# Shared expert of three token groups computed in the drain of the attention, and the whole shared expert in plain fp32

## The reference, cut to what matters

```python
def _L1_ffn_ref(hidden_tensor, w_router, w1_stack, w2_stack, ws1, ws2):
    ...   # two experts of eight for each token, weighted: moe_out
    sh = jnp.square(jax.nn.relu(jnp.einsum('btc,fc->btf', hidden_tensor, ws1)))
    shared_out = jnp.einsum('btf,cf->btc', sh, ws2)
    return shared_out + moe_out
...
t = t + _L1_ffn_ref(_ln_t(t), L1_ffn_w_router, L1_ffn_w1_stack, L1_ffn_w2_stack, L1_ffn_ws1, L1_ffn_ws2)
```

## Time and profile before

| what | value |
|---|---|
| median of three runs | 1196.7 us |
| profiled execution | 1199.71 us |
| its span, first to last instruction | 1197.3 us |
| mean granted clock of TensorE, share of full speed | 0.920 |
| PE busy, matmuls | 1025.8 us (86%) |
| DVE busy | 615.7 us (51%) |
| ACT busy | 528.2 us (44%) |
| POOL busy | 264.1 us (22%) |
| DMA | 114.61 MB, mean 96 GB/s |

### The profile page before, as it was taken

One profiled execution on the slowest core, in us unless ns is written; L12 is line 12 of the kernel. 1 busy time (PEld: TensorE's weight loads), 2 busy tenths in 40 slices (PEclk: granted clock), 3 DMA queues, 4 the chain that ended last, 5 costly groups with the idle time before them and its releaser, 6 DMA issues. The chain is left out here.

```text
span 1197.3 us, 19835 instructions
## 1 busy us (share of the span) xinstructions
PE 1025.8 (86%) x5686; PEld 858.5 (72%) x5686; DVE 615.7 (51%) x1712; ACT 528.2 (44%) x1328; POOL 264.1 (22%) x274
## 2 busy tenths in 40 slices
PE   6956669999999999973489999998776799997897
PEld 6956658888888888862256665665535799986787
DVE  5488653323232322226356676555778355554566
ACT  6027264444444444432144344433335466666563
POOL 0000012111111111107522200000000554424655
PEclk9999999999999999995689999997665799998889
DMA  9533501111111111118222301002230344434444
GB/s 354 234 110 136 176 24 49 53 54 54 54 54 53 54 54 54 49 41 268 73 80 79 89 1 53 36 18 71 89 123 1 101 139 140 136 114 150 151 131 132
DMA packets 63237, 114.61 MB, mean 96 GB/s; under 512 B 9827, under 2 KB 43253, under 8 KB 62262
## 3 DMA queue, kind: packets, MB, share of 16 engines
q1 hardware_dynamic: 49910, 77.65, 18.5%
q0 software_dynamic: 12960, 35.41, 10.4%
q10 hardware_dynamic: 288, 0.47, 0.1%
HBM read 73.90 MB, written 39.59 MB: 95 GB/s over the span
## 5 line engine op out<-in xcount | busy, mean ns | idle before, releaser
L574 POOL DMA_INDIRECT experts_rows_sb<-h_rows,ids_i x142 | 134.6, 948 | 751.0 <-POOLq L402 423.1
L761 DVE TENSOR_TENSOR experts_a_sb<-experts_a_sb,experts_bankU 128x512 f32<-128x512 f32 x71 | 48.9, 689 | 224.1 <-PE experts_bankU L180 224.1
L714 ACT ACTIVATE experts_a_sb<-experts_bankG 128x512 f32<-128x512 f32 (+1 forms) x142 | 70.0, 493 | 93.0 <-PE experts_bankG L180 91.2
L705 ACT ACTIVATE experts_hT<-experts_bankH 128x256 fp32r<-128x256 f32 x142 | 54.5, 384 | 89.6 <-PE experts_bankH L634 89.5
L727 ACT ACTIVATE experts_y_sb<-experts_bankY 128x256 f32<-128x256 f32 x142 | 54.8, 386 | 87.7 <-PE experts_bankY L177 65.3
L178 PE MATMUL attn_bankC<-attn_padded,attn_w_high 128*128 128x512 f32 x144 | 76.4, 530 | 19.8 <-ACT attn_feat L1432 14.6
L1136 POOL DMA_INDIRECT attn_y<-y_rows,pos_i x64 | 63.9, 998 | 112.2 <-DVE x_res L1562 57.2
L834 POOL DMA_INDIRECT shared_y<-y_rows,pos_i x64 | 65.4, 1022 | 63.9 <-DVE x_res L943 32.1
L177 PE MATMUL experts_bankY<-down_plain,experts_aT_plain 128*128 x284 | 72.9, 379 | 0.0
L183 DVE TENSOR_TENSOR experts_aT<-experts_bankA,experts_aT 128x256 fp32r<-128x256 f32 x142 | 59.6, 420 | 24.1 <-ACT experts_aT L722 24.1
L641 PE MATMUL experts_bankA<-konst_sb,experts_a_sb 128*128 128x128 f32 x426 | 70.0, 273 | 0.4 <-DVE experts_aT L183 0.4
(11 more groups left out here) (365 smaller groups left out, 2853.5 us busy)
## 6 DMA issues: line engine op xcount, KB each, us to landing
y_rows<-experts_y_sb SPq DMA_DIRECT2D x142, 128.0 KB, 1.7
h_rows<-xn SPq DMA_DIRECT2D x32, 256.0 KB, 2.4
x_res<-in_x SPq DMA_DIRECT2D x4, 1024.0 KB, 12.3
mix_xT<-in_xt SPq DMA_DIRECT2D x4, 1024.0 KB, 14.1
gate_raw<-in_L_ffn_gate_w SPq DMA_DIRECT2D x1, 4096.0 KB, 14.2
up_raw<-in_L_ffn_up_w SPq DMA_DIRECT2D x1, 4096.0 KB, 23.5
x_rows<-x_res SPq DMA_DIRECT2D x16, 256.0 KB
x_res<-x_rows SPq DMA_DIRECT2D x8, 512.0 KB, 4.6
```

The lines of the kernel that those rows point to most:

```text
L574: nc.gpsimd.indirect_dma_start(rows[t % DEPTH][:, :], None, h_dram, bass.IndirectOffsetOnAxis(ap=ids_i[:, t:t + 1], axis=0)).then_inc(s_ro ...
L714: nc.scalar.activation(a_sb[i % RING][:, :], bankG[i % RING][:, 0:hidden], ACT.Silu if gate is not None else ACT.Relu).then_inc(s["act"], 1)
L761: nc.vector.tensor_tensor(a_sb[i % RING][:, :], a_sb[i % RING][:, :], bankU[i % RING][:, 0:hidden], ALU.mult).then_inc(s["a"], 1)
```

## The change

- PE, ACT and DVE compute the shared expert of pairs 4, 5 and 6 (`EARLY`) inside `attention`. In iteration i PE multiplies the turned rows of pair i-5, which lie in `xT` for the router, by `ws1` (`shared_up`, four chunks, in banks that the attention no longer uses), ACT takes relu and square (`activate_shared`), and in iteration i+1 PE multiplies back (`shared_down`, four tiles) and DVE adds the result to `x_res` in two halves (`add_shared`). This falls into iterations 9 to 12. Their rows aren't stored to `ht_dram`.
- `ws1` and `ws2` are loaded as they are by two DMAs in iteration 8 and never split; 16 pieces are left, and `SHARES` falls to one in each of iterations 10 to 12.
- `shared` does the other five groups. All its products are single plain fp32 matmuls; there is no high or low half of rows, weights or activations. The five groups of rows have a buffer each and are loaded at the start. There are 16 gather buffers. The tiles are gathered, summed and stored in the order of groups 4, 0, 1, 5, 2, 6, 3, 7; a tile of an early group needs only its two sums.

```diff
+GROUP = 4
+EARLY = (4, 5, 6)
 ...
         def shared(ws1, ws2):
-            GROUPS = TILES // GROUP
+            LATE = [g for g in range(TILES // GROUP) if g not in EARLY]
+            SEQUENCE = [t for g in (4, 0, 1, 5, 2, 6, 3, 7) for t in range(g * GROUP, (g + 1) * GROUP)]
-            DEPTH = 8
+            DEPTH = 16
 ...
-                            last = product(bankU[k][:, :], [w[:, kc * IS + k * P:kc * IS + (k + 1) * P] for w in ws1],
-                                           [x[:, kc * N:(kc + 1) * N] for x in hT[g % RING]], kc == 0, kc == KC - 1)
+                            last = nc.tensor.matmul(bankU[k][:, :], ws1[0][:, kc * IS + k * P:kc * IS + (k + 1) * P], hT[n][:, kc * N:(kc + 1) * N],
+                                                    start=(kc == 0), stop=(kc == KC - 1))
 ...
-                            last = product(bankY[t % GROUP][:, 0:C], [x[:, at:at + P] for x in aT[g % RING]],
-                                           [w[:, k * C:(k + 1) * C] for w in ws2], k == 0, k == KI - 1)
+                            last = nc.tensor.matmul(bankY[m % GROUP][:, 0:C], a[n % RING][k][:, m % GROUP * P:(m % GROUP + 1) * P],
+                                                    ws2[0][:, k * C:(k + 1) * C], start=(k == 0), stop=(k == KI - 1))
 ...
+                        if t // GROUP not in EARLY:
+                            dve.wait_ge(s["down"], late(t) + 1)
+                            dve.wait_ge(s["sum"], n * 2 + 2)
+                            nc.vector.tensor_tensor(x_tile(t), x_tile(t), bankY[t % GROUP][:, 0:C], ALU.add).then_inc(s["added"], 1)
 ...
         def attention(on):
-            SHARES = {0: 3, 1: 3, 2: 2, 8: 3, 9: 2, 10: 2, 11: 2, 12: 3}
+            SHARES = {0: 3, 1: 3, 2: 2, 8: 3, 9: 2, 10: 1, 11: 1, 12: 1}
 ...
+                    if i == PAIRS:
+                        sp.wait_ge(s["conv"], PAIRS)
+                        sp.dma_start(ws1[0][:, :], A["L1_ffn_ws1"]).then_inc(s["s_weights"], 16)
+                        sp.dma_start(ws2[0][:, :], A["L1_ffn_ws2"]).then_inc(s["s_weights"], 16)
 ...
-                    if has(i - 5):
+                    if has(i - 5) and i - 5 not in EARLY:
 ...
+                def shared_up(p, k):
+                    if p not in EARLY:
+                        return
+                    c = EARLY.index(p) * KI + k
+                    bank = (bankF, bankS["down"])[k % 2]
+                    pe.wait_ge(s["s_weights"], 2 * 16)
+                    pe.wait_ge(s["f_copied"], p * 2 + 2)
+                    if c >= 2:
+                        pe.wait_ge(s["s_relu"], c - 1)
+                    else:
+                        pe.wait_ge(s[("along_sb", "att_sb")[k]], PAIRS)
+                    for kc in range(KC):
+                        last = nc.tensor.matmul(bank[:, :], ws1[0][:, kc * IS + k * P:kc * IS + (k + 1) * P], xT[:, kc * 512:(kc + 1) * 512],
+                                                start=(kc == 0), stop=(kc == KC - 1))
+                    last.then_inc(s["s_up"], 1)
+
+                def shared_down(p, t):
+                    ...
+                    bank = (bankC, bankQ)[t // 2]
+                    pe.wait_ge(s["s_square"], (n + 1) * KI)
+                    ...
+                    for k in range(KI):
+                        last = nc.tensor.matmul(bank[:, t % 2 * C:(t % 2 + 1) * C], shared_a[k][:, t * P:(t + 1) * P], ws2[0][:, k * C:(k + 1) * C],
+                                                start=(k == 0), stop=(k == KI - 1))
+                    if t % 2:
+                        last.then_inc(s["s_down"], 1)
 ...
                     turn_rows(i - 5, 0)
+                    shared_down(i - 6, 0)
                     gate_layer(i - 2, 1)
                     convolve(i, 5, 7)
                     turn_rows(i - 5, 1)
+                    shared_down(i - 6, 1)
                     gate_layer(i - 2, 2)
                     convolve(i, 7, 8)
+                    shared_down(i - 6, 2)
                     scores(i - 1, "down")
 ...
                     gate_layer(i - 2, 3)
+                    shared_down(i - 6, 3)
 ...
                     branch(i)
+                    shared_up(i - 5, 0)
                     gate_layer(i - 2, 5)
 ...
                     turn_logits(i - 5)
+                    shared_up(i - 5, 1)
 ...
                     turn_gated(i - 2)
+                    shared_up(i - 5, 2)
 ...
                     attend_along(i - 2)
+                    shared_up(i - 5, 3)
 ...
-                        act.wait_ge(s_turned_out, p * 16)
+                        if p - 1 in EARLY:
+                            act.wait_ge(s["s_up"], (EARLY.index(p - 1) + 1) * KI)
+                        else:
+                            act.wait_ge(s_turned_out, sum(g not in EARLY for g in range(p)) * 16)
 ...
                     gate_exp(i - 2)
+                    activate_shared(i - 5, 0)
 ...
                     copy_along(i - 1)
+                    activate_shared(i - 5, 1)
                     copy_gated(i - 2)
+                    for k in range(2, KI):
+                        activate_shared(i - 5, k)
 ...
                     row_stats(i - 4, 3)
+                    add_shared(i - 6, 0)
 ...
                     bound(i - 2)
+                    add_shared(i - 6, 1)
```

More of the change, by code:

```diff
@@ L839, in _ @@
                 def _(sp):
[L840 to L852, removed]
+                    for n, g in enumerate(LATE):
+                        sp.dma_start(hT[n][:, :], ht_dram[:, g * KC * N:(g + 1) * KC * N]).then_inc(s_turned[n], 16)
+                    for n, t in enumerate(SEQUENCE):
+                        if t // GROUP in EARLY:
+                            sp.wait_ge(s["sum"], n * 2 + 2)
+                        else:
+                            sp.wait_ge(s["added"], late(t) + 1)
+                        sp.dma_start(out[t * P:(t + 1) * P, :], x_tile(t)).then_inc(s["stored"], 16)
                     sp.wait_ge(s["stored"], TILES * 16)
@@ L882, in _ @@
                         project(c)
[L883 to L885 removed]
+                    for m in range(len(LATE) * GROUP):
+                        project_back(m)
+                        project(m + LEAD)
                 @block.scalar
                 def _(act):
[L890 to L896 removed]
@@ L898, in activate @@
-                    def activate(c):
-                        g, k = c // KI, c % KI
+                    for c in range(len(LATE) * KI):
+                        n, k = c // KI, c % KI
                         act.wait_ge(s["up"], c + 1)
-                        if g:
-                            act.wait_ge(s["a_low"], c - KI + 1)
-                        nc.scalar.activation(a[k][:, :], bankU[k][:, :], ACT.Relu).then_inc(s["relu"], 1)
+                        if n >= RING:
+                            act.wait_ge(s["down"], (n - RING + 1) * GROUP)
+                        nc.scalar.activation(a[n % RING][k][:, :], bankU[k][:, :], ACT.Relu).then_inc(s["relu"], 1)
@@ L913, in _ @@
[L913 to L916 removed]
+                        nc.scalar.activation(a[n % RING][k][:, :], a[n % RING][k][:, :], ACT.Square).then_inc(s["square"], 1)
                 @block.vector
                 def _(dve):
[L921 to L925 removed]
@@ L983, in attention @@
             s_turned_out = sem("moe1_turned_out")
+            s.update({f"s_{n}": sem(f"shared_early_{n}") for n in ("weights", "up", "relu", "square", "down", "added")})
             for ax in AXES:
@@ L995, in attention @@
                 w_half = [w_high, sb("attn_w_low", [P, STEPS * F], HALF, on=early, side="right")]
-            for held, name, width in ((down1, "down1", E * I1 // P * C), (ws1, "ws1", KC * IS), (ws2, "ws2", IS // P * C)):
-                held.extend(halves_of(name, width))
+            down1.extend(halves_of("down1", E * I1 // P * C))
+            for held, name, width in ((ws1, "ws1", KC * IS), (ws2, "ws2", IS // P * C)):
+                held.append(sb(name, [P, width], side="right"))
+            KI = IS // P
+            shared_a = [sb(f"attn_shared_a{k}", [P, 512], on=on, side="right") for k in range(KI)]
             step = 512
@@ L1000, in attention @@
             pieces = [(A[name][:, at:at + step], high[:, at:at + step], low[:, at:at + step])
-                      for name, (high, low) in (("L1_ffn_w1_stack", up1), ("L1_ffn_w2_stack", down1), ("L1_ffn_ws1", ws1), ("L1_ffn_ws2", ws2))
+                      for name, (high, low) in (("L1_ffn_w1_stack", up1), ("L1_ffn_w2_stack", down1))
                       for at in range(0, high.shape[1], step)]
@@ L1753, in normalise_rows, with add_shared @@
                         last.then_inc(s["f_xn"], 1)
+                def add_shared(p, half):
+                    if p not in EARLY:
+                        return
+                    dve.wait_ge(s["s_down"], EARLY.index(p) * 2 + half + 1)
+                    x2 = x_tile(p * PT + half * 2, n=2)
+                    nc.vector.tensor_tensor(x2, x2, (bankC, bankQ)[half][:, :], ALU.add).then_inc(s["s_added"], 1)
```

115 lines of the change are left out of this document (40 added, 75 removed).

## The result

The changed kernel took 1211.3 us (median of 4 runs, 1202.5 to 1214.4); the kernel before, on the same chip, 1199.0 (median of 4, 1191.8 to 1201.6). The ratio is 1.0117, with a 95% interval of 1.0076 to 1.0159: slower by 1.2%, where 1192, about no change, was forecast. The profiled execution has a span of 1210.9 us, 13.6 more than before.

A forecast was written before the change was run, and what follows sets the result against it. PE was taken to lead the last stage, with POOL becoming its bound. The profile's 1199.7 - 30.2 (last stage) + 25.4 (drain) = 1194.9 us, or 1192 against the median; range 1177 to 1214.

The forecast's parts named there:

- Prices on PE: fp32 shared expert on PE: an up 1.72 us, a down 1.73; 110 us for the whole, against 90 before.
- four passes at a rounded product's price each: Alternative fp32 price on PE, from the skill: 0.93 and 0.47 us a product, drain below 3 us longer; not adopted.
- The drain: Attention iterations 9 to 12 take on 41.3 us of PE products and lengthen by 25.4 us.
- the clock's 2.6: Drain: rest of the first ups and start of iteration 10 pay double at the low clock, +2.6 us.
- Rival B: Drain: the low clock stays in iterations 9 and 10, 20.6 us more, so 1213; whole drain low 1236; 19%.
- POOL becomes the bound. End: 1167.1, 30.2 us earlier: Last stage: 64 gathers 1.29 us apart on POOL, last starting at 1160.3, plus 6.8 us to the end.
- PE leads: Last stage before the change, 119 us: PE busy for 99.6, POOL waiting for DVE's sums, which follow PE.
- The sum: Whole kernel: 1199.7 - 30.2 + 25.4 = 1194.9 us against the profile, 1192 against the median.
- D: Last stage: gathers keep their mean distance of 1.77 us, set by something other than free buffers; no gain, 1222; 3%.
- or a PE that is the bound after all: Sign against the forecast: POOL waiting for DVE in the last stage would mean gathers keeping their distance, or PE as bound.
- few gathers last much above 0.95 us: Argument that POOL's gathers in the trace are not held up by DVE holding the ports they share.

The follow-up runs named there:

- e4: Changed kernel with no group moved: all eight groups of the shared expert in fp32 in the last stage; 1191.6 us, ratio 0.9961.
- e18: Changed kernel, unchanged, run on another chip, where PE's updates come promptly; 1178.8 us, ratio 1.0100.
- e2: Kernel before with only the first 8 of the 64 gathers of its last stage, DVE summing all tiles from those; 1183.1 us.
- e17: Kernel before with a 256-column memset on POOL after every fourth gather in last stage and attention, repeated on another prompt chip; 1170.7 us, ratio 1.0032.
- e10: Changed kernel, unchanged, run again on a late chip; 1212.5 us, ratio 1.0107.
- e12: Changed kernel with a memset of 1.0 us on POOL after every fourth gather of the last stage, on a late chip; 1214.9 us.

## Why the prediction was wrong

- **Prices on PE: right.** An "up" starts 1.72 us after the one before it, a "down" 1.73, in every undisturbed stretch. The whole in one stage took 112 us for 110 forecast (e4). By the row of the Trainium skill that I set beside it (FP8 and Floating Point Precision, TensorE Precision Notes), four passes at a rounded product's price each, it would be an estimated 120; the trace does not agree with that price.
- **The drain: right in mechanism, a little low.** Iteration 9 took 4.2 us more than before's 17.0 (forecast 4.4), iteration 10 19.9 (18.0), iteration 11 18.9 (17.8), iteration 12 to the keep 13.0 (12.5). In the first pair the clock's 2.6 were not paid, since the clock was 1.00 from 860 on; where it rose later they were: in e18 it was 0.54 from 833 to 844 and 0.66 from 856 to 861, and iterations 9 and 10 took 23.2 and 21.6. The drain with all that precedes the first gather is 287.9 us in the first trace; over eight traces of kernels with three groups moved it is 291.4, over six with the drain of before 262.1: +29, forecast +25.4, 25.2 in the first pair. Rival B, the low clock that stays, is dead: units beside the gate layers ran at the full clock, which fits the rule cited there (the Trainium skill, TensorE: Matmul & The Clock Gate, What's actually happening).
- **"POOL becomes the bound. End: 1167.1, 30.2 us earlier": the step that failed.** The step takes a stage of 118.3 us as PE's own work and pace ("PE leads") and lets all of it go but what POOL needs, 88.1. On a prompt chip the second number is right (86.4 in e18), but the stage to compare with is some 102: the move gives 16 us. On a late chip the 118.3 is real, but some 16 us of it come with the gathers (e2: 102.2 with eight of them), and these stay: the new stage took 104.1 and 104.7, and the move gives 13 to 14. The lateness did not go with PE's work, and in the new stage it costs a little more, 18 us (104.4 less 86.4): fewer products and 16 buffers let 26 gathers run without a pause, where before the longest runs were 12 to 14. On either kind of chip the term was about twice its size.
- **The sum.** In the first pair of traces the stage gives 14.2 us instead of 30.2, the drain takes 25.2, and the convolution ended 2.6 us later: +13.6. Late chips in the mean: stage 117.6 to 104.4, -13; drain +25 to +33; measured +12 and +13. Prompt chips: stage some 102 to 86.4, -16; drain +29; measured +12. That 102 is an estimate, since no trace of the kernel before is from a prompt chip: e17's 106.2 less the 4 us by which its pauses lengthen the whole kernel. The two kinds of chip agree on the change, 1.0 to 1.2% slower.
- **Of the rivals** none was it. D named gathers that keep their distance, because of something other than free buffers. The gathers kept 1.25; it was the others that waited for them. I said that the forecast is wrong if POOL waits for DVE in the last stage "or a PE that is the bound after all": both happened, as consequences. No rival had a signal that arrives late. B's 1213 stands near the measured 1211.3 by chance: the low clock did not stay. Against D I said that few gathers last much above 0.95 us; in the kernel before 16 of 64 lasted over 1.1. No run shows whether that is the lock that was cited there, and the distance of 1.27 in e18 rules out D all the same.
- **What the profile of before would have told.** The row of L903 has 16.5 us "<-remote", and PE was held inside products twice, for some 4 us each. I quoted that row for another number. It says that ACT waited for something that no engine's work was just ending, so that the stage was not simply PE's; how much shorter it would be without that, only a run like e2 tells.

## What to carry to other kernels

Before a stage's length is used as one side of a difference, split it: busy time, waits whose releaser has just ended, and waits that end when nothing does ("remote", "issue" inside a product). The last kind belongs to no engine that the change makes faster, and it may grow when the engine that causes it is given more room. And where deeper buffers let a stream of gathers run free, look at what the others do meanwhile.

## What the runs showed of the hardware

- During runs of gathers 1.25 us apart waiters for PE's semaphore updates started up to 18 us after the modelled end of the work that makes them (17.7 in the first trace and 18.2 in e10; the sum over 20 is 105 and 108 us). Every trace from the chips on which the kernel before took 1195 us or more has them beside the attention's gathers too, where its longest "remote" wait is 11 to 24 us (the ten traces from prompt chips have none), and in the last stage where gathers run on there; with eight gathers (e2), or a memset of 1.0 us after every fourth (e12), the last stage had none. On other chips the changed kernel, with the same gathers, had only the floor of 6.1 (e18). The Trainium skill (Advanced Engine Details and Errata, Network/Comms) gives 50 to 100 ns for reading a semaphore's value from a sequencer. No run here times such a read; in e18 most relus start 0.04 us after the modelled end of their chunk.
- In the convolution PE itself loses time by it. From 560 to 620, beside the attention's gathers, the kernel before on a late chip (first) and the changed one on a prompt chip (second), by busy time:

```profile
560.00:620.00 60.00, 36.67 (x122) 23.61 (x121) 24.14 (x80) 13.28 (x35) 29.29 (x30) 0.72 0.34 103
```

```profile
560.00:620.00 60.00, 49.18 (x195) 34.10 (x195) 35.94 (x117) 22.82 (x61) 35.20 (x34) 0.89 0.44 136
```

  The convolution ends at 816 to 819 in the one kind of trace (808 to 810 in three of them) and at 796 to 800 in the other. With the 16 us of the last stage that accounts for about the 29 to 34 us between the two kinds of chip for the kernel before.
- On late chips the traces also miss update records. The changed kernel left 8793 and 8841 of them there (first trace, e10) and 12759 in e18, with 19300 instructions recorded in each. In block 1's experts 21 of PE's 71 updates for a finished output bank stand in the trace of before, and all 71 in e18. But nothing is late there: ACT's copies of that bank start 8.4 us after its modelled ends, summed over 71, and 7.5 in e18, and the stage takes 141 us either way. So a missing record is not a late update; lateness above is taken from when the waiter starts.
- Not settled: what makes a chip late. No run separates the chip itself, work on its other cores, and the recording of traces. The missing records go with late chips in every trace, which makes the recording a suspect, and no more than that. The Trainium skill (NOTIFIC — the notification-queue block, 7.1 Overflow: three behaviours, one of which stalls the engine) says that the block that records events can hold engines back; no run here shows it.
